# An attention and expert layer on one core: fewer counts for SP, and POOL's and VectorE's work around the last tiles laid out anew

## The chip, the core and the metric

One core of one Trainium2 chip runs the program. The metric is the device time of one execution in microseconds (us). The number to predict is the median for the changed kernel; for the kernel before it is 307.4 us.

## What is computed

x holds 2 x 1024 tokens of 256 numbers, the context 2 x 64 rows of 256, all in float32. The reference, cut to what matters:

```python
def attention(q_in, kv_in):            # 16 heads of 64; scores / sqrt(64), softmax over 64 keys
    q, k, v = q_in @ Wq + bq, kv_in @ Wk + bk, kv_in @ Wv + bv
    return softmax(q @ k.T / 8) @ v @ Wo + bo

def ffn(x):                            # 2048 tokens, 8 experts, 2 chosen for each token
    scores = sigmoid(x @ W_router)
    _, sel = top_k(scores + expert_bias, 2)
    w = scores[sel] / sum(scores[sel])
    shared = silu(x @ Wg_s) * (x @ Wu_s) @ Wd_s
    routed = [silu(x @ Wg[e]) * (x @ Wu[e]) @ Wd[e] for e in sel]
    return shared + sum(w * routed)

x = x + tanh(g_xattn) * attention(layernorm(x), ctx)
x = x + tanh(g_ffn) * ffn(layernorm(x))
```

The expert biases spread widely, so most tokens go to the same two experts.

## The kernel before

The tokens are 16 tiles of 128 rows. Each engine runs its own program; semaphores tie them. VectorE is `dve` (DVE), ScalarE `act`, TensorE `pe`, GpSimd `pool` (POOL), and SP issues most of the DMAs. An order of work is written out by hand on every engine.

**Start.** Wq and K are folded into matrices A and V and Wo into matrices B, one pair of heads after the other (`fold_v` on TensorE, L1392). V lies first in two PSUM banks, one for each half of the head pairs. `finish_v` adds the bias and copies it into `vT`: the first half on VectorE in two instructions (L988), the second on ScalarE in eight (L764), signalled by `v_done`. Each pair's B goes to SBUF as a high part (ScalarE, L736) and a low part (VectorE, L998). VectorE also makes the statistics of the first layer norm, in batches (`norm_stats`, L966 and L969).

**Token loop.** In step t the engines work on several tiles: scores of tile t + 2; row maximum and subtraction on VectorE (L1150, L1156), the exponential on ScalarE (L771), row sum and reciprocal of tile t + 1 on VectorE (L1140, L1144), multiplication with the reciprocal on POOL (L648), transposition and the attention product of tile t on TensorE, the second norm, and the shared expert of tile t - 2. Of the latter, `hidden(v)` gates the rows: for the tiles of `BY_POOL` (3 to 11) POOL does it from copies that ScalarE makes (L600, L602; the copies are L791 and L794), for the others VectorE from PSUM (L1095, L1098). In the step T - 3 = 13, VectorE's `choose(3)` picks the experts of tiles 9 to 11 after `hidden`; L1030 and L1031 are the smaller and the larger of two expert numbers.

POOL also scatters the normalized rows of each tile into the experts' areas in DRAM, twice per tile (`put_tile`, L612), from step 6 on; in step 13 it scatters tile 7, multiplies, gates tile 11 and scatters tile 8.

**Before the experts.** TensorE does the shared expert's down product of twelve tiles (`late_transpose`, `late_down`), among them `rank(6)`, a product for the totals and `count`. VectorE waits for these (L1051), fills `tables()` (which expert each of the 39 tiles of 128 slots belongs to, and what SP is to gather), gates tile 15 and makes the low parts of half of Wd (L1239); POOL had made the other half in the loop (L667).

**Experts.** Each engine runs 39 tiles, eight tiles unrolled in a hardware loop and the first and last steps written out. SP gathers the rows of tile j + 4 in step j (L504), after VectorE has written the scatter index of tile j (L1312); POOL scatters each tile's result to `routed_dram` (L691). When all tiles that hold rows of a part of the tokens are scattered, their results can be loaded. Four parts of four token tiles are loaded twice: plane 0 holds each token's result of the lower-numbered expert, plane 1 that of the higher (`load_plane`, L408, 512 KB each). How far the scatters must be for each of the eight loads is computed by VectorE in steps 1 and 2 (`last_turns`, `count_turns`), and SP reads it into registers, four for each load:

```python
for k, first in enumerate((4, 32)):
    if isinstance(j, int) and first <= j < first + T // PLANE:
        sp.wait_ge(chunk_turns_done, 1)
        turns.append(turn_values(chunk_turns[0:1, k, j - first, :]))
```

So steps 4 to 7 read the four rows of plane 0 and steps 32 to 35 the four of plane 1. At the end VectorE adds plane 0 (L1283, `add_low`) and plane 1 (L1331) for tiles 0 to 11, TensorE and ScalarE do tiles 12 to 15, and SP and ScalarE store (L402).

## Time and profile before

| | |
|---|---|
| median of 3 runs | 307.4 us (306.29 to 309.32) |
| the profiled execution, its own time | 309.48 us |
| its span in the profile | 307.7 us |
| mean granted clock of TensorE, share of full speed | 0.989 |
| TensorE matmul busy | 278.0 us (90%) |
| VectorE busy | 241.7 us (79%) |
| POOL busy | 170.0 us (55%) |
| ScalarE busy | 163.9 us (53%) |

The busy times say how much each engine has to do, not what sets the end. The chain of waits is followed back from the last instruction, at each step to what released it. A row in a timeline gives the start in us, how long it took (a merged row spans several instructions, their number behind the x), the engine, the line, what is written and read, and in brackets how long the engine was idle before and who ended that.

### The profile page before, as it was taken

Reading aid. Unit: us, or ns where it says so; the run is one execution under the profiler, and the core shown is the slowest. Engines: PE = TensorE matmul, PEld = TensorE weight load, DVE = VectorE, ACT = ScalarE, POOL = GpSimd, SP = SyncE. Lnnn points to the kernel's source line nnn. Section 1 sums busy time; section 2 is a strip of 40 time slices with the busy share of each in tenths; the row PEclk is TensorE's granted clock in tenths of the full one; section 3 lists DMA queues with packets and bytes.
Section 4 is the critical chain, followed back from the end, with each engine's and each line's share of the span. In section 5 each row is a group of like instructions: output and inputs, shape, how many; then the busy total and the mean of one; then the engine's idle time right before and its main releaser. Section 6 shows DMA issues by size and latency. Waiting matters only on the chain.

```text
span 307.7 us, 6608 instructions
## 1 busy us (share of the span) xinstructions
PE 278.0 (90%) x1746; PEld 248.8 (81%) x1747; DVE 241.7 (79%) x687; ACT 163.9 (53%) x426; POOL 170.0 (55%) x236
## 2 busy tenths in 40 slices
PE   2999979999999899999986969987799999999992
PEld 1788757898897798999876948876799899999881
DVE  0489869999999699989999575778877777777755
ACT  1462785666756566673653434744355565657611
POOL 8012216787757876897886775409553444444520
PEclk9999999999999999999998897999999999999999
DMA  6999994133379999713031122313244434343697
GB/s 186 367 295 318 269 293 119 47 90 94 102 207 292 306 315 325 223 36 105 35 104 37 53 87 88 90 53 105 69 123 126 118 92 121 113 129 105 223 344 264
DMA packets 45006, 49.74 MB, mean 162 GB/s; under 512 B 3928, under 2 KB 41650, under 8 KB 44978
## 3 DMA queue, kind: packets, MB, share of 16 engines
q1 hardware_dynamic: 39938, 39.37, 44.4%
q0 software_dynamic: 3408, 8.46, 8.1%
q10 hardware_dynamic: 1632, 1.57, 1.5%
q8 instruction: 13, 0.21, 0.3%
q14 instruction: 15, 0.12, 0.1%
HBM read 21.67 MB, written 28.64 MB: 163 GB/s over the span
## 4 chain that ended last, share of the span: by engine, by line
PE 47%; DVE 26%; issue 9%; DMA 6%; ACT 6%; POOL 3%; SPq 1%; DVEq 0%; ACTq 0%; POOLq 0%
PE bank L1404 5%; PE bank L1406 4%; PE bank L1405 4%; PE scores_ps L1404 4%; DVE probs L1156 4%; PE scores_ps L1406 3%; DVE pT_lo L1133 3%; DVE row_sum L1140 3%; PE scores_ps L1405 3%; PE bank L1350 3%; DMA Wk_sb<-in_L_xattn_Wk_dram 3%; DMA AB_free<-routed_dram 2%; DVE row_max L1150 2%; PE bank L1601 2%; PE scores_ps L1441 2%
## 5 line engine op out<-in xcount | busy, mean ns | idle before, releaser
L691 POOL DMA_INDIRECT routed_dram<-probs,sct_idx x39 | 38.0, 975 | 57.1 <-ACT probs L915 55.6
L648 POOL TENSOR_TENSOR probs<-probs,row_inv 128x1024 f32<-128x1024 f32 x16 | 30.5, 1908 | 25.2 <-DVE row_inv L1144 24.9
L612 POOL DMA_INDIRECT rows_dram<-xn,slot_i x32 | 32.0, 1001 | 14.6 <-issue 11.2
L1404 PE MATMUL bank<-AB_hi,pT_hi 128*128 128x256 f32 x128 | 37.7, 294 | 2.2 <-DVE pT_lo L1133 2.2
L1406 PE MATMUL bank<-AB_hi,pT_lo 128*128 128x256 f32 x128 | 36.5, 285 | 0.0
L1405 PE MATMUL bank<-AB_lo,pT_hi 128*128 128x256 f32 x128 | 36.4, 285 | 0.0
L771 ACT ACTIVATE probs<-probs 128x1024 f32<-128x1024 f32 x16 | 16.9, 1058 | 29.6 <-DVE probs L1156 29.6
L1404 PE MATMUL scores_ps<-AB_hi,xnT_hi 128*128 128x512 f32 x64 | 26.4, 413 | 1.8 <-DVE xnT_lo L1126 1.7
L1404 PEld LDWEIGHTS bank<-AB_hi,pT_hi 128*128 128x128 f32 x128 | 24.9, 194 | 2.7 <-issue 2.5
L1406 PE MATMUL scores_ps<-AB_hi,xnT_lo 128*128 128x512 f32 x64 | 25.3, 396 | 0.0
L1405 PE MATMUL scores_ps<-AB_lo,xnT_hi 128*128 128x512 f32 x64 | 25.3, 395 | 0.0
L1405 PEld LDWEIGHTS bank<-AB_lo,pT_hi 128*128 128x128 f32 x128 | 24.9, 194 | 0.0
L1406 PEld LDWEIGHTS bank<-AB_hi,pT_lo 128*128 128x128 f32 x128 | 24.8, 193 | 0.0
L1133 DVE TENSOR_TENSOR pT_lo<-bank,pT_hi 128x512 fp32r<-128x512 f32 x32 | 20.5, 682 | 1.8 <-ACT pT_hi L779 1.4
L1150 DVE TENSOR_REDUCE row_max<-scores_ps 128x16 f32<-128x1024 f32 x16 | 19.1, 1196 | 1.7 <-PE scores_ps L1406 1.6
L1302 DVE TENSOR_TENSOR xnT_lo<-bank,xnT_hi 128x256 fp32r<-128x256 f32 x39 | 16.6, 425 | 3.9 <-ACT xnT_hi L892 2.9
L1156 DVE TENSOR_TENSOR probs<-scores_ps,row_max 128x1024 f32<-128x1024 f32 x16 | 19.4, 1216 | 0.1
L1140 DVE TENSOR_REDUCE row_sum<-probs 128x16 f32<-128x1024 f32 x16 | 19.4, 1210 | 0.1
L830 ACT ACTIVATE xn2T_hi<-bank 128x256 fp32r<-128x256 f32 x16 | 6.2, 385 | 22.6 <-PE bank L1474 20.0
L1503 PE MATMUL bank<-ident,probs 128*128 128x128 f32 x128 | 16.9, 275 | 1.1 <-POOL probs L648 1.0
L779 ACT ACTIVATE pT_hi<-bank 128x512 fp32r<-128x512 f32 x32 | 17.2, 594 | 1.0 <-PE bank L1503 0.9
L1404 PE MATMUL bank<-W_hi,xnT_hi 128*128 x40 | 15.5, 387 | 2.0 <-DVE xnT_lo L1302 2.0
(249 smaller groups left out, 886.4 us busy)
## 6 DMA issues: line engine op xcount, KB each, us to landing
rows_dram<-pad_rows SPq DMA_DIRECT2D x10, 1040.0 KB, 15.8
rows_dram<-pad_rows SPq DMA_DIRECT2D x8, 780.0 KB, 12.5
AB_free<-routed_dram SPq DMA_DIRECT2D x8, 512.0 KB, 7.9
probs<-rows_dram SPq DMA_DIRECT2D x30, 130.0 KB
raw_buf<-in_L_ffn_Wg_dram SPq DMA_DIRECT2D x8, 192.0 KB, 2.5
raw_buf<-in_L_ffn_Wu_dram SPq DMA_DIRECT2D x8, 192.0 KB, 2.9
out_dram<-x_sb ACTq DMA_DIRECT2D x6, 256.0 KB, 2.7
pT_hi<-rows_dram SPq DMA_DIRECT2D x9, 130.0 KB
```

The costliest lines, as they stand in the source:

```text
L612: nc.gpsimd.indirect_dma_start(rows_dram[:, :], bass.IndirectOffsetOnAxis(ap=slot_i[:, t, k:k + 1], axis=0), xn2[:, t % KEEP, :], None).th ...
L648: nc.gpsimd.tensor_tensor(pr, pr, row_inv[:, :].unsqueeze(2).to_broadcast([P, H, KV]), ALU.mult).then_inc(norm_done, 1)
L691: nc.gpsimd.indirect_dma_start(routed_dram[:, :], bass.IndirectOffsetOnAxis(ap=sct_idx[(k - 2) % (2 * RING)][:, 0:1], axis=0), y_sb[ks][:, ...
L771: nc.scalar.activation(prob[m % 2][:, :], prob[m % 2][:, :], ACT.Exp).then_inc(exp_done, 1)
L779: nc.scalar.activation(pT_hi[:, 4 * h:4 * h + 4, :], pT_ps[h][:, :].rearrange("p (c s) -> p c s", c=4), ACT.Copy).then_inc(pT_hi_done, 1)
L1133: nc.vector.tensor_tensor(pT_lo[:, 4 * h:4 * h + 4, :], pT_ps[h][:, :].rearrange("p (c s) -> p c s", c=4), pT_hi[:, 4 * h:4 * h + 4, :].bi ...
L1140: nc.vector.tensor_reduce(row_sum[:, :], prob[m % 2][:, :].rearrange("p (h k) -> p h k", k=KV), AX_X, ALU.add).then_inc(sum_done, 1)
L1150: nc.vector.tensor_reduce(row_max[:, :], by_head, AX_X, ALU.max).then_inc(max_done, 1)
L1156: nc.vector.tensor_tensor(prob[u % 2][:, :].rearrange("p (h k) -> p h k", k=KV), by_head, row_max[:, :].unsqueeze(2).to_broadcast([P, H, KV]),
L1404: nc.tensor.matmul(out_ap, a_hi, b_hi, start=first, stop=False)
L1405: nc.tensor.matmul(out_ap, a_hi, b_lo, start=False, stop=False)
L1406: return nc.tensor.matmul(out_ap, a_lo, b_hi, start=False, stop=last)
```

## The change

Five edits:

1. SP keeps five rows of turns, not eight. The four of plane 0 are read in steps 4 to 7 as before. The readings of steps 32 to 35 are gone; the fifth row (the turn after which everything is scattered) is read after plane 0's third load and holds for all four loads of plane 1. `chunk_slots` and `chunk_turns` shrink to match.
2. VectorE computes these counts in steps 1, 2 and 3 of the experts and not in 1 and 2.
3. `BY_POOL` ends at tile 9: `hidden` of tiles 10 and 11 is VectorE's, from PSUM, and ScalarE's copies for them go. In step 13 `choose(3)` stands before `hidden`. POOL's scatters of tiles 7 to 9 move: in step 13 tile 7 and one half of tile 8 after the multiplication, then the other half in step 14 before it and tile 9 after it.
4. V's second half is VectorE's as well (`finish_v(1)`, two instructions), directly after the first; the third batch of statistics moves from there to a place after the row maximum of tile 1.
5. Before the experts: `rank(6)`, the totals and `count` stand ahead of `late_down(2)` on TensorE; `hidden(15)` stands ahead of the wait for the count on VectorE; the two late subtractions for Wd go from VectorE to POOL, after the tables.

```diff
-BY_POOL = range(3, 12)
+BY_POOL = range(3, 10)
...
-                for k, first in enumerate((4, 32)):
-                    if isinstance(j, int) and first <= j < first + T // PLANE:
-                        sp.wait_ge(chunk_turns_done, 1)
-                        turns.append(turn_values(chunk_turns[0:1, k, j - first, :]))
+                if isinstance(j, int) and 4 <= j < 4 + T // PLANE:
+                    sp.wait_ge(chunk_turns_done, 1)
+                    turns.append(turn_values(chunk_turns[0:1, j - 4, :]))
...
                     n = k * (T // PLANE) + c
+                    if n == T // PLANE - 1:
+                        turns.append(turn_values(chunk_turns[0:1, T // PLANE, :]))
                     for r in range(RING):
-                        sp.wait_ge(scattered[r], turns[n][r])
+                        sp.wait_ge(scattered[r], turns[min(n, T // PLANE)][r])
...
-                if 6 <= t < T - 2:
+                if 6 <= t < T - 3:
                     put_tile(t - 6)
                 if t == T - 2:
-                    put_tile(9, [0])
+                    put_tile(8, [1])
...
                 if t == T - 3:
-                    put_tile(8)
+                    put_tile(7)
+                    put_tile(8, [0])
                 if t == T - 2:
-                    put_tile(9, [1])
+                    put_tile(9)
...
+            pool.wait_ge(tile_row_done, 1)
+            for n in (2, 3):
+                part = slice(4 * n, 4 * n + 4)
+                pool.wait_ge(wd_hi_done, n + 1)
+                nc.gpsimd.tensor_tensor(Wd_lo[:, part, :], raw_d[n % 2][:, :, :, :].rearrange("p e k d -> p (e k) d"),
+                                        Wd_hi[:, part, :].bitcast(F32), ALU.subtract).then_inc(wd_lo_late, 1)
...
-            finish_v(1)
             high_x(2)
...
+                if t == T - 3:
+                    choose(3)
                 if inside(v) and v not in BY_POOL:
                     hidden(v)
-                if t == T - 3:
-                    choose(3)
...
             finish_v(0)
-            dve.wait_ge(ld_x[2], 16)
-            norm_stats(range(*NORMS[2]))
+            finish_v(1)
...
             max_rows(1)
+            dve.wait_ge(ld_x[2], 16)
+            norm_stats(range(*NORMS[2]))
             B_low([2])
...
             choose(6)
+            hidden(T - 1)
             dve.wait_ge(count_ps_done, 1)
             place(6, last=True)
             tables()
-            hidden(T - 1)
...
-                        pe.wait_ge(v_done, 2 * GC)
+                        pe.wait_ge(kv_done, 4 * NG)
...
-            late_down(2)
             rank(6)
             nc.tensor.matmul(last_ps, ones_r[:, :], mask[:, :, :].rearrange("p t e -> p (t e)"), start=True, stop=True)
             count(range(*BATCHES[6]), count_ps_done)
+            late_down(2)
```

The end of SP's program before, from the last row of turns on. `chunk_turns` are the counts, `AB_free` the planes; L487 is a reading of one value.

```order
L487 TENSOR_LOAD chunk_turns [waits chunk_turns_done]
L487 ISA x2
L487 TENSOR_LOAD chunk_turns
L487 ISA x2
L487 TENSOR_LOAD chunk_turns
L487 ISA x2
L487 TENSOR_LOAD chunk_turns
L487 ISA x2
L408 DMA AB_free<-routed_dram 128x4x256 [waits scattered2,scattered3,scattered1,scattered0] x4
L408 DMA AB_free<-routed_dram 128x4x256 [waits scattered3,scattered2,late_added,scattered1,scattered0] x4
L402 DMA out_dram<-x_sb 128x2x256 [waits plane1_added] x2
```

Now, from the last gather on (the numbers of the lines are almost the same there).

```order
L504 DMA probs<-rows_dram 128x260
L408 DMA AB_free<-routed_dram 128x4x256 [waits scattered2,scattered3,scattered1,scattered0] x3
L487 TENSOR_LOAD chunk_turns
L487 ISA x2
L487 TENSOR_LOAD chunk_turns
L487 ISA x2
L487 TENSOR_LOAD chunk_turns
L487 ISA x2
L487 TENSOR_LOAD chunk_turns
L487 ISA x2
L408 DMA AB_free<-routed_dram 128x4x256 [waits scattered2,scattered3,scattered1,scattered0]
L408 DMA AB_free<-routed_dram 128x4x256 [waits scattered3,scattered2,late_added,scattered1,scattered0] x4
```

The readings no longer stand between the last gather and the loads; four remain, behind the third load.

POOL from the multiplication of step 12 to that of step 13, before.

```order
L648 TENSOR_TENSOR probs<-probs,row_inv 128x1024 [waits inv_done]
L600 TENSOR_TENSOR gate_act<-tanh_g,late_hid 128x192 [waits plus_one_done,h_read,hid_done]
L602 TENSOR_TENSOR late_hid<-gate_act,late_hid 128x192 [waits gact_done]
L667 TENSOR_TENSOR AB_lo<-raw_buf,AB_hi 128x512 [waits wd_hi_done]
L626 TENSOR_TENSOR ve<-mv,eps_col 128x1 [waits xn2_done,mv2_done]
L627 TENSOR_TENSOR neg_mean<-mv,minus_one 128x1
L629 TENSOR_TENSOR rstd<-ve,minus_half 128x1 [waits ln2_step]
L631 TENSOR_TENSOR shift<-neg_mean,rstd 128x1 [waits ln2_step]
L612 DMA rows_dram<-xn,slot_i 16512x260 [waits filled2,xn2_done,payload_done,slot_done]
L612 DMA rows_dram<-xn,slot_i 16512x260 [waits xn2_done]
L648 TENSOR_TENSOR probs<-probs,row_inv 128x1024 [waits inv_done]
L600 TENSOR_TENSOR gate_act<-tanh_g,late_hid 128x192 [waits plus_one_done,h_read,hid_done]
```

The same stretch now (L649 is the multiplication, L613 the scatter).

```order
L649 TENSOR_TENSOR probs<-probs,row_inv 128x1024 [waits inv_done]
L668 TENSOR_TENSOR AB_lo<-raw_buf,AB_hi 128x512 [waits wd_hi_done]
L627 TENSOR_TENSOR ve<-mv,eps_col 128x1 [waits xn2_done,mv2_done]
L628 TENSOR_TENSOR neg_mean<-mv,minus_one 128x1
L630 TENSOR_TENSOR rstd<-ve,minus_half 128x1 [waits ln2_step]
L632 TENSOR_TENSOR shift<-neg_mean,rstd 128x1 [waits ln2_step]
L649 TENSOR_TENSOR probs<-probs,row_inv 128x1024 [waits inv_done]
L613 DMA rows_dram<-xn,slot_i 16512x260 [waits filled2,xn2_done,payload_done,slot_done]
L613 DMA rows_dram<-xn,slot_i 16512x260 [waits xn2_done]
L613 DMA rows_dram<-xn,slot_i 16512x260 [waits filled3,xn2_done,payload_done,slot_done]
L627 TENSOR_TENSOR ve<-mv,eps_col 128x1 [waits xn2_done,mv2_done]
```

The gating (L600, L602) is gone, and the two scatters stand behind the second multiplication.

VectorE at the start, around the row maximum of tile 1, before.

```order
L998 SCALAR_TENSOR_TENSOR AB_lo<-bank,tgate,AB_hi 128x2x256 [waits B_hi_done,gates_done]
L1150 TENSOR_REDUCE row_max<-scores_ps 128x16 [waits sub_done,scores_done]
L998 SCALAR_TENSOR_TENSOR AB_lo<-bank,tgate,AB_hi 128x2x256 [waits B_hi_done,gates_done]
L1156 TENSOR_TENSOR probs<-scores_ps,row_max 128x1024 [waits max_done]
L998 SCALAR_TENSOR_TENSOR AB_lo<-bank,tgate,AB_hi 128x2x256 [waits B_hi_done,gates_done]
L998 SCALAR_TENSOR_TENSOR AB_lo<-bank,tgate,AB_hi 128x2x256 [waits B_hi_done]
```

And now (L994 is the low part of B, L1146 the maximum, L962 and L965 the statistics).

```order
L994 SCALAR_TENSOR_TENSOR AB_lo<-bank,tgate,AB_hi 128x2x256 [waits B_hi_done,gates_done]
L1146 TENSOR_REDUCE row_max<-scores_ps 128x16 [waits sub_done,scores_done]
L962 BN_STATS stats<-x_sb 128x6 [waits ld_x2]
L962 BN_STATS stats<-x_sb 128x6 x2
L965 BN_AGGR mv<-stats 128x2 [waits stats1_done] x3
L994 SCALAR_TENSOR_TENSOR AB_lo<-bank,tgate,AB_hi 128x2x256 [waits B_hi_done,gates_done]
L1152 TENSOR_TENSOR probs<-scores_ps,row_max 128x1024 [waits max_done]
L994 SCALAR_TENSOR_TENSOR AB_lo<-bank,tgate,AB_hi 128x2x256 [waits B_hi_done,gates_done]
```

The three statistics stand between the maximum and the low part of pair 2.

## Rows read from the trace of the kernel before

**Rows 1.** The page, part 4: the chain, share of the span by engine.

```profile
PE 47%; DVE 26%; issue 9%; DMA 6%; ACT 6%; POOL 3%; SPq 1%; DVEq 0%; ACTq 0%; POOLq 0%
```

**Rows 2.** The chain in order of time, 28 to 50 us: start, us, what.

```profile
35.77 0.24 ACT vT L764
```

**Rows 3.** Timeline, 28 to 41 us: start, us, engine, line, op, [idle before].

```profile
27.98 1.37 DVE L988 TENSOR_TENSOR vT<-bank,bias_cols 64x512 f32<-64x512 f32 x2
...
29.38 1.08 DVE L966 BATCH_NORM_STATS2 stats<-x_sb 128x6 f32<-128x256 f32 x3
...
30.38 0.30 DVE L969 BATCH_NORM_AGGREGATE mv<-stats 128x2 f32<-128x6 f32 x3
...
35.67 3.07 ACT L764 ACTIVATE vT<-bank,bias_cols 64x128 f32<-64x128 f32 x8
...
36.75 1.21 DVE L1150 TENSOR_REDUCE row_max<-scores_ps 128x16 f32<-128x1024 f32 x1
...
39.96 0.75 DVE L998 SCALAR_TENSOR_TENSOR AB_lo<-bank,tgate,AB_hi 128x512 fp32r<-128x512 f32 x1 [1.99 <-ACT AB_hi L736]
```

**Rows 4.** Timeline of POOL, then DVE, 156 to 170 us; last, line L1030 alone.

```profile
159.21 1.92 POOL L648 TENSOR_TENSOR probs<-probs,row_inv 128x1024 f32<-128x1024 f32 x1
...
156.88 0.25 DVE L1144 RECIPROCAL row_inv<-row_sum 128x16 f32<-128x16 f32 x1
...
158.71 2.46 DVE L1030 TENSOR_TENSOR bank<-top_e 128x3 f32<-128x3 uint32 x1
...
161.71 1.21 DVE L1150 TENSOR_REDUCE row_max<-scores_ps 128x16 f32<-128x1024 f32 x1
...
168.66 0.29 DVE L1095 SCALAR_TENSOR_TENSOR gate_act<-tanh_g,bank 128x192 f32<-128x192 f32 x1
168.99 0.35 DVE L1098 TENSOR_TENSOR late_hid<-gate_act,bank 128x192 f32<-128x192 f32 x1
...
L1030 DVE TENSOR_TENSOR bank<-top_e x7: 168/172/2459, 87.4 to 187.6; 128x3 f32<-128x3 uint32 x4, 128x1 f32<-128x1 uint32 x2, 128x2 f32<-128x2 uint32 x1
```

**Rows 5.** Timeline, 186 to 203 us; ahead of it line L667 alone.

```profile
L667 POOL TENSOR_TENSOR AB_lo<-raw_buf,AB_hi x4: 1286/1288/1298, 128.1 to 153.9; 128x512 fp32r<-128x512 f32 x4
...
189.82 0.17 DVE L1051 TENSOR_TENSOR hot_val<-hot,bank 128x16 f32<-128x16 f32 x1 [1.51 <-PE bank L1453]
...
196.32 2.35 DVE L1239 TENSOR_TENSOR AB_lo<-raw_buf,AB_hi 128x1024 fp32r<-128x1024 f32 x2
...
201.80 0.38 PE L1601 MATMUL bank<-ident,probs 128*128 128x128 f32 x2
```

**Rows 6.** Timeline of SP, 274 to 294 us, and one row of DVE.

```profile
274.95 6.22 SPq L504 DMA_DIRECT2D probs<-rows_dram  x3
286.17 7.42 SPq L408 DMA_DIRECT2D AB_free<-routed_dram  x8
...
278.95 0.21 DVE L1312 SCALAR_TENSOR_TENSOR sct_idx<-probs,tile_e 128x1 int32<-128x1 f32 x1
```

**Rows 7.** The chain in order of time, 283 us to the end.

```profile
284.89 3.99 DMA routed_dram<-probs,sct_idx
...
288.97 7.35 DMA AB_free<-routed_dram
```

**Rows 8.** Timeline of DVE, 292 us to the end.

```profile
292.86 0.29 DVE L1103 TENSOR_TENSOR pT_lo<-bank,pT_lo 64x128 fp32r<-64x128 f32 x1
296.35 1.67 DVE L1331 SCALAR_TENSOR_TENSOR x_sb<-AB_free,weight,x_sb 128x256 f32<-128x256 f32 x4 [3.19 <-DMA AB_free<-routed_dram]
...
302.69 1.67 DVE L1331 SCALAR_TENSOR_TENSOR x_sb<-AB_free,weight,x_sb 128x256 f32<-128x256 f32 x4
```

**Rows 9.** Tile AB_free, landings; then the DMA view of 284 to 304 us.

```profile
DMA to landing us min/median/max: 5.2/7.9/9.2
...
GB/s 180 82 0 0 66 144 88 326 367 326 350 311 335 287 295 338 295 291 379 377 385 349 350 328 324 334 348 338 349 312 330 377 363 297 272 358 350 313 88 348
...
out_dram<-x_sb ACTq DMA_DIRECT2D x6, 256.0 KB, 2.7
```

43 lines of the change are left out of this document (16 added, 27 removed).

## The prediction, made before the changed kernel had run

> **What bounds the kernel now.** I read the chain by engine first: half of the span's chain is TensorE and a quarter VectorE [rows 1], so no engine alone sets the end and a saving counts only where its own piece of the chain is. The chain in order of time therefore decides. Four places of it touch the change.
>
> At 35.77 us the chain runs through ScalarE's V copies [rows 2]: eight of them hold ScalarE for 3.07 us, and VectorE idles 1.99 us in front of the low part at 39.96 us for a high part that ScalarE makes only after them [rows 3].
>
> In step 13 of the token loop VectorE is the chain. One 128x3 minimum of `choose(3)` (L1030) takes 2.46 us, from 158.71 to 161.17; POOL's multiplication of the probabilities (L648) runs from 159.21 to 161.13, and both end together [rows 4]. The row maximum behind it starts at 161.71.
>
> Between the token loop and the experts VectorE idles 1.51 us for the count of TensorE, then makes the tables, then two low parts of Wd in 2.35 us; the third tile's transposition starts at 201.80 [rows 5]. VectorE's late work there is behind the tables and TensorE is busy with the late products all the while, so it is not on the chain.
>
> The end: SP issues its last gathers from 274.95 to 281.17 us, and its first plane load only at 286.17 [rows 6]. What the first plane loads wait for was there long before. Counting the routing of the reference's own inputs, the experts get 1943, 28, 2048, 0, 0, 0, 0 and 77 rows, thus 16, 1, 16 and 1 tiles, 34 of the 39; plane 0's four loads need 21, 25, 29 and 33 tiles, and each of plane 1's four needs all 34. So only SP's reading of turns stands between the gathers and the loads: eight readings in 5.00 us, 0.62 us each. Plane 1's first load is issued at 288.97, when the scatter that was started at 284.89 has landed, and lands 7.35 us later [rows 7]. VectorE is ready for it at 293.15, waits 3.19 us, and then adds without a gap: 296.35 to 304.36 [rows 8]. In that time the DMA engines move some 335 GB/s almost from the first plane load on [rows 9]: plane 1 lands late because 2.1 MB of plane 0 are ahead of it.
>
> **The change part by part**, against the profiled execution (309.48 us, of which 307.7 are span; the median of the runs shown is 307.4, and I carry the sum over to it).
>
> SP's turns. All three steps of 32 to 35 lose their readings: sixteen of them go (10 us of SP's time), four come back as row 5, behind plane 0's third load. The last gather needs the index that VectorE writes at 278.95 + 0.21 = 279.16 [rows 6]; so the gathers end near 279.6 and the first three loads of plane 0 (each 0.52 MB, at 335 GB/s 1.57 us, together 4.7 us) go out about 6 us earlier and have landed by some 287. The four readings of row 5 (2.5 us, until 283.8) are covered, since plane 0's fourth load needs tile 33, whose scatter lands one tile before 288.9. Plane 1's first load cannot start before 288.97: both ways its count is 34. What is new is that the queue ahead of it holds at most the fourth load. A store of half the size takes 2.7 us from issue to landing [rows 9], of which 0.8 is the moving at 335 GB/s; so 0.52 MB alone take 1.9 + 1.57 = 3.5 us, and it lands at 292.5. VectorE is free at 293.15 only, so its adds start 296.35 - 293.2 = 3.15 us earlier. Bounds: nothing, if landing takes 7.35 us again; 2.15, if it takes the shortest of the eight (5.2 us, 294.2) [rows 9]; 3.2 at most, because then VectorE's own work ends it. I take **-3.1**, since the bytes ahead are what made it long. What follows is the same 20 adds and the same last stores, and those of TensorE's and ScalarE's tail move by as much.
>
> V on VectorE. Two instructions for the second half cost what the first two did, 1.37 us, and stand where three statistics stood (1.08 + 0.30 = 1.38) [rows 3]: nothing before the first row maximum moves. The statistics go behind the second maximum, which ends at 36.75 + 1.21 = 37.96; with 1.38 more VectorE reaches the low part at 39.3 instead of 39.96. ScalarE has lost 3.07 us, so its high part should be there. **-0.6**; bounds nothing (the high part still late) and -1.99 (all of the idle time).
>
> The gated rows of tiles 10 and 11. VectorE gets two instructions a tile, 0.29 + 0.35 and their gaps, 0.72 us [rows 4], once in step 12 and once in step 13; ScalarE loses two copies and POOL two products in each. Step 12 is a VectorE-bound round, so +0.7. In step 13 POOL now multiplies before it scatters: it can start once the reciprocal of 156.88 is there, later by the 0.7, so near 157.9, and ends near 159.8. `choose(3)` reaches L1030 at 158.71 + 0.7 = 159.4 and is held 0.4 us, not 2.3. Added: +0.7 + 0.7 - 2.0 = -0.6. POOL's scatters of tiles 7 to 9 then crowd toward step 15 by some tenths, and TensorE's idle time after rank(3) changes little. I take **-0.4**; bounds -2 (the gated rows fall into idle time) and +1.4 (the stall stays).
>
> Why the 128x3 minimum waits is a matter of a shared port. Both its inputs lie in SBUF. The Trainium skill (SBUF — State Buffer, "Who interferes with whom") says that such an instruction contends with a GpSimd instruction that reads SBUF, and that the one issued first keeps the port to its end. The trace agrees on the end (161.17 against 161.13) but not on the order: VectorE's began 0.5 us before POOL's. By the rule VectorE would have gone first and the stall would be chance; by the row it belongs to POOL's next instruction. With either the new order leaves 0.4.
>
> Before the experts. TensorE's rank and count go ahead of `late_down(2)`, so VectorE's idle 1.51 us takes in the gated rows of tile 15 and the tables end about 0.6 us sooner; TensorE's late products themselves stay, so this is worth nothing by itself. The Wd subtractions on POOL: its halves took 1.29 us for 512 columns [rows 5], so 1024 take at most 2 x 1.29 = 2.58, two 5.2. They wait for the tables, which end before VectorE's gated rows (0.7) and its own subtractions of 196.32, and now 0.6 sooner: from about 195.0 to 200.2. TensorE asks for them ahead of the transposition of 201.80: 1.6 us in hand, cost nothing, or up to 1 us if the port slows POOL. Behind them in POOL's queue are only the late adds, and nobody waits for those before the planes.
>
> Counts over three steps: nine instructions in steps 1 and 2 become nine in 1, 2 and 3. SP wants them at step 4. Half of what leaves steps 1 and 2 comes back in step 3, where VectorE waits for ScalarE anyway: **-0.1**, between -0.5 and +0.3.
>
> Sum: -3.1 - 0.6 - 0.4 - 0.1 = -4.2. That is 305.3 for an execution like the profiled one, and for the median 307.4 - 4.2 = **303.2 us**.
>
> **The rivals.**
> 1. The tail gives less: plane 1's four loads share the engines and the first lands as late as before. For it: they are issued close together, and 7.35 us is the only value seen for this load. Against it: then four loads were ahead. With 7.35 the tail gives nothing, 307.4 - 1.1 = 306.3; with 5.2 it would be 304.2.
> 2. The stall in step 13 stays, because POOL's other work (three scatters behind the multiplication) holds the port as well. Then the loop costs +1.4 and not -0.4: 303.2 + 1.8 = 305.0. Against it: of seven such minima only this one took over 0.2 us or so (the median is 0.172) [rows 4].
> 3. Slower: the early loads of plane 0 hold up the last tiles' scatters. The scatter of tile 34 took 3.99 us; if the 4.7 us of plane 0's bytes were ahead of it, it would land at 293.6, plane 1's first load would land at 293.6 + 7.35 = 301.0 in place of 296.3, and the end would be 4.7 - 1.1 = 3.6 us later: 311.0. It decides when more than about a third of these bytes still lie ahead at 284.89. Against it: they were issued from 279.7 and should be nearly through, and in the trace of before three loads were issued 1.3 us after that scatter without spoiling it.
> 4. The change does not do what it says: SP's readings stay between gathers and loads. The order excludes it.
>
> **How the numbers follow.** Forecast 0.68, rival 1 0.17, rival 2 0.10, rival 3 0.05. The range: below, the sum with V at -1.0, the loop at -1.4 and the tail at -3.2, 301.2; above, it reaches to rival 1, which with its noise I cut at 306.2. One per cent of 307.4 is 3.1 us, about what a measurement of this kernel can tell from no change: faster by more needs under 304.3. The forecast lies 1.1 below that, and the runs shown scatter by 3 us, so nine tenths of its chance count as faster, and a part of rival 1; rival 2 is no change. Faster 0.69, same 0.27, slower 0.04.
>
> **What would show it.** SP's first plane load near 279.7, a gap of 0.6 us from the last gather; VectorE's wait at L1331's new line near nothing, at about 292; L1030's successor at 0.5 us or less; no idle time over 1.5 us before the low part near 39; TensorE without a wait for POOL at 200. If the sum of the tail is under 1.5 us, or the step from 152 to 172 us is longer than before, the forecast is wrong.

## The result and the profile after

Twenty executions of each kernel: before 308.44 us median (306.29 to 309.47), changed 305.95 us (304.95 to 309.23). The ratio of the two is 0.9929, 95% interval 0.991 to 0.9948, so 2.2 us faster (1.6 to 2.8), where 4.2 were forecast. The time lies inside the range of 301.2 to 306.2, by a quarter of a microsecond, but 2.75 us above the forecast of 303.2. One of these comes from the start: the median of three runs (307.4) was a microsecond under the one of twenty. The forecast gave 0.69 to a gain of over one per cent (under 304.3) and 0.27 to no such change; the second came. Half of the expected gain was eaten, and this part is about by what.

VectorE's rows at the start, after the change:

```profile
36.63 0.67 DVE L994 SCALAR_TENSOR_TENSOR AB_lo<-bank,tgate,AB_hi 128x512 fp32r<-128x512 f32 x1
37.25 1.23 DVE L1146 TENSOR_REDUCE row_max<-scores_ps 128x16 f32<-128x1024 f32 x1
38.39 1.07 DVE L962 BATCH_NORM_STATS2 stats<-x_sb 128x6 f32<-128x256 f32 x3
39.37 0.30 DVE L965 BATCH_NORM_AGGREGATE mv<-stats 128x2 f32<-128x6 f32 x3
39.59 0.73 DVE L994 SCALAR_TENSOR_TENSOR AB_lo<-bank,tgate,AB_hi 128x512 fp32r<-128x512 f32 x1
```

The idle 1.99 us of [rows 3] is gone; the statistics fill 1.2 of it. The first row maximum came at 31.28 and not 30.71, but it varies by more than that without the V part too (below). In step 13 (VectorE, then POOL):

```profile
150.10 1.22 DVE L1146 TENSOR_REDUCE row_max<-scores_ps 128x16 f32<-128x1024 f32 x1
...
158.94 0.45 DVE L1026 TENSOR_TENSOR bank<-top_e 128x3 f32<-128x3 uint32 x1
```

```profile
157.45 1.91 POOL L649 TENSOR_TENSOR probs<-probs,row_inv 128x1024 f32<-128x1024 f32 x1 [2.46 <-DVE row_inv L1140]
```

The minimum takes 0.45 us where [rows 4] had 2.46. The end, SP, then VectorE, then TensorE's last products before and after:

```profile
278.42 11.60 SPq L408 DMA_DIRECT2D AB_free<-routed_dram  x8
299.26 1.17 SPq L402 DMA_DIRECT2D out_dram<-x_sb  x2
```

```profile
292.02 1.67 DVE L1328 SCALAR_TENSOR_TENSOR x_sb<-AB_free,weight,x_sb 128x256 f32<-128x256 f32 x4 [0.38 <-DMA AB_free<-routed_dram]
...
298.36 1.66 DVE L1328 SCALAR_TENSOR_TENSOR x_sb<-AB_free,weight,x_sb 128x256 f32<-128x256 f32 x4
```

```profile
300.91 0.70 PE L1445 MATMUL bank<-AB_free,late_hid 128*128 128x256 f32 x2 [1.18 <-DMA AB_free<-routed_dram]
...
302.31 0.59 PE L1445 MATMUL bank<-AB_free,late_hid 128*128 128x256 f32 x2
```

```profile
297.67 1.03 PE L1442 MATMUL bank<-AB_free,late_hid 128*128 128x256 f32 x4
...
299.40 0.59 PE L1442 MATMUL bank<-AB_free,late_hid 128*128 128x256 f32 x2
```

The first plane load is issued at 278.42 (286.17 in [rows 6]) and the adds start at 292.02 (296.35 in [rows 8]). Counted from the last scatter index (287.51 before, 285.99 now), VectorE's last add ends 14.03 us later where it was 16.84, but TensorE's last product 14.0 us later where it was 15.4: before, VectorE ended last by 1.5 us; now both end level. So each place that the forecast named did what it said, and the time still went elsewhere. Two views show where to look. TensorE's rows in front of the last rank (line 1459 is `rank(6)`'s first product, 1438 `late_down`):

```profile
185.59 0.38 PE L1431 MATMUL bank<-ident,late_hid 128*96 128x128 f32 x2
186.88 0.27 PE L1459 MATMUL bank<-mask,upper 128*128 128x8 f32 x1 [0.91 <-DVE mask L1038]
```

And the windows of 160 to 190 us, before and then after (columns: length, busy PE, PEld, DVE, ACT, POOL, granted clock of TensorE, DMA share, GB/s):

```profile
160.00:175.00 15.00, 11.27 (x73) 10.39 (x72) 11.71 (x28) 5.12 (x14) 10.82 (x17) 0.89 0.11 40
175.00:190.00 15.00, 11.99 (x68) 10.22 (x67) 9.26 (x54) 5.71 (x17) 10.25 (x14) 0.89 0.26 90
```

```profile
160.00:175.00 15.00, 12.62 (x75) 11.83 (x74) 10.94 (x27) 5.38 (x15) 10.35 (x16) 0.77 0.15 55
175.00:190.00 15.00, 11.67 (x72) 9.87 (x72) 11.29 (x65) 5.96 (x20) 11.23 (x16) 1.00 0.26 90
```

A mean of 0.89 over 15 us is 3.4 us at the lower of TensorE's two levels (1.2 GHz); 0.77 is 6.9 us. Such stretches are 3.4 us long here, or twice that, and how many fall, and where, differs between executions of one kernel, so a pair of traces must first be compared on them. The table does that for the profiled executions of all kernels with a whole tail. Its times are differences of starts in VectorE's timeline: the first to the third row maximum, the 14th to the 15th, the 15th to the 16th, the 14th to the first scatter index; then from the last scatter index to the end of the span. "Low" counts the 3.4 us stretches between 155 and 200 us; where there is one, it begins at 164.6 to 166.3, where there are two, the second begins at 181 to 185, or one of double length stands for both (changed, from 165.1; order only, from 180.4).

| kernel | 1st to 3rd | 14th to 15th | 15th to 16th | 14th to index | low | tail |
|---|---|---|---|---|---|---|
| before | 18.35 | 7.74 | 11.78 | 58.22 | 2 | 20.19 |
| changed | 17.40 | 8.33 | 10.48 | 57.37 | 2 | 18.21 |
| changed, again | 17.41 | 8.34 | 10.47 | 56.89 | 1 | 18.75 |
| turns only | 18.33 | 7.73 | 11.79 | 55.43 | 0 | 18.51 |
| old turns | 17.40 | 8.33 | 10.47 | 56.89 | 1 | 20.71 |
| V only | 17.40 | 7.74 | 11.78 | 56.26 | 1 | 20.29 |
| rows only | 18.36 | 8.33 | 10.47 | 57.16 | 2 | 20.89 |
| order only | 18.36 | 7.74 | 9.74 | 57.20 | 2 | 22.28 |
| late moves only | 18.39 | 7.74 | 11.76 | 56.32 | 0 | 21.57 |
| late product back | 17.40 | 8.34 | 10.46 | 55.97 | 1 | 18.66 |
| POOL's order | 17.40 | 8.34 | 10.47 | 56.90 | 2 | 18.54 |
| one row back | 17.40 | 7.74 | 10.40 | 54.92 | 1 | 17.94 |

The first row maximum itself stands anywhere from 29.06 to 31.64 us in these, with and without the V part; the loads of the first 30 us are the likely cause, which no run singles out. The place of a stretch counts as well: in three runs of the tail below, whose token loop is the changed kernel's, the way from the 14th row maximum to the first index is 57.9 us with one stretch from 180 to 182 us on, against 56.89 with one at 165, and 57.87 with both. So two rows of the table compare well only where number and place are alike. For the pair of the first two rows the pieces add up: +0.57 at the start, -0.95, -0.04 (third to 14th), -0.85, -0.25 (between the first and the last index), -1.98, together the 3.5 us between the spans 307.7 and 304.2. The profiled execution of before was the slowest of its twenty, which is most of why the pair says 3.5 and the ratio 2.2.

### The profile page after: what moved, and what is told of

Same layout as the page of the kernel before. It is cut to its first block, busy times and chain, and to the rows that moved or that the text cites. A ratio compares the mean times of both kernels' runs of the same rounds, so it can differ in the third digit from the quotient of the medians.

```text
span 304.2 us, 6562 instructions
## 1 busy us (share of the span) xinstructions
PE 277.8 (91%) x1746; PEld 249.2 (82%) x1747; DVE 239.6 (79%) x691; ACT 159.8 (53%) x414; POOL 172.9 (57%) x234
## 4 chain that ended last, share of the span: by engine, by line
PE 54%; DVE 26%; issue 7%; ACT 5%; POOL 3%; DMA 3%; SPq 1%; DVEq 0%; ACTq 0%; POOLq 0%
PE bank L1401 6%; PE bank L1403 5%; PE bank L1402 5%; PE scores_ps L1401 4%; PE scores_ps L1403 4%; PE scores_ps L1402 4%; DVE pT_lo L1129 4%; DVE probs L1152 4%; DVE row_sum L1136 3%; PE bank L1347 3%; DVE row_max L1146 3%; DMA Wk_sb<-in_L_xattn_Wk_dram 3%; PE bank L1598 2%; PE scores_ps L1438 2%; PE bank L1438 2%
## 5 line engine op out<-in xcount | busy, mean ns | idle before, releaser
L649 POOL TENSOR_TENSOR probs<-probs,row_inv 128x1024 f32<-128x1024 f32 x16 | 30.5, 1909 | 25.8 <-DVE row_inv L1140 25.6
L613 POOL DMA_INDIRECT rows_dram<-xn,slot_i x32 | 32.0, 1001 | 12.5 <-issue 10.5
L1299 DVE TENSOR_TENSOR xnT_lo<-bank,xnT_hi 128x256 fp32r<-128x256 f32 x39 | 16.5, 424 | 8.1 <-ACT xnT_hi L888 7.1
L1146 DVE TENSOR_REDUCE row_max<-scores_ps 128x16 f32<-128x1024 f32 x16 | 19.2, 1200 | 1.6 <-PE scores_ps L1403 1.6
L1401 PEld LDWEIGHTS scores_ps<-AB_hi,xnT_hi 128*128 128x128 f32 x64 | 12.0, 188 | 6.8 <-DVE xnT_lo L1122 4.7
```

Source lines behind the costliest of these rows:

```text
L613: nc.gpsimd.indirect_dma_start(rows_dram[:, :], bass.IndirectOffsetOnAxis(ap=slot_i[:, t, k:k + 1], axis=0), xn2[:, t % KEEP, :], None).th ...
L649: nc.gpsimd.tensor_tensor(pr, pr, row_inv[:, :].unsqueeze(2).to_broadcast([P, H, KV]), ALU.mult).then_inc(norm_done, 1)
L1146: nc.vector.tensor_reduce(row_max[:, :], by_head, AX_X, ALU.max).then_inc(max_done, 1)
L1401: nc.tensor.matmul(out_ap, a_hi, b_hi, start=first, stop=False)
```

## The experiments

Every ratio is to the kernel before on the same chip. The expectations argue by theories. 1: the pieces of the profiled pair, with TensorE's tail as the new bound of the end. 2: the late product that was moved had covered a wait. 3: POOL's queue takes back what VectorE wins. 4: TensorE and VectorE hold the end together. 5: one gated row is better left on POOL. 6: the DMA engines hold the end as well. They count tiles from 0, so their row maximum 15 is the 16th here.

**Turns alone.** The kernel before with the first part of the change (five rows, `turns[min(n, T // PLANE)]`, `tiles_up_to`, `last_turns`, `count_turns`):

```diff
-                        sp.wait_ge(scattered[r], turns[n][r])
+                        sp.wait_ge(scattered[r], turns[min(n, T // PLANE)][r])
```

> The kernel before with the five rows of turns and the counts over three steps, nothing else. Theory 1 (TensorE's tail is the new bound): the experts end when they did, VectorE's first add of plane 1 starts some 2.8 us earlier (near 293.5), but TensorE's four late products and twelve sums run without a wait from the end of the experts, lose only their own wait of 1.18 us for plane 1, and the span is 2.0 us shorter (305.7), ratio near 0.9935. Rival 1 (the prediction's step: TensorE's and ScalarE's tail move with VectorE's adds): 2.8 to 3.1 us shorter (304.7), ratio 0.990 to 0.991. Rival 2 (the medians, not the profiled pair, are right, and the early plane loads cost the scatters of the last tiles something in most executions): 1 us or less, ratio 0.997, with the last scatter landing 0.6 us later than 3.99 us after its issue.

Ratio 0.9937 (0.9903 to 0.9971), 305.32 against 307.28 us. This is theory 1's number, though the interval touches the prediction's (0.990 to 0.991); the trace decides. The tail is 18.5 us, and from the last scatter index VectorE's adds end at 14.3 us (16.8 before), TensorE's products at 14.1 (15.4 before). Over the six profiles of the table with the old turns the tail is 20.2 to 22.3 us, mean 21.0, over the six with the new ones 17.9 to 18.75, mean 18.4: 2.0 us in the profiled pair, 2.5 in the means.

**Old turns, the rest as changed.**

> The changed kernel with the old eight rows of turns and counts over two steps. Theory 1: only the lead of the experts is left, 1.5 us (third tile's gather, transpositions and the scatters 1.5 earlier), VectorE waits again about 3.2 us for plane 1's first load, and the span is 1.5 us shorter than before (306.2), ratio near 0.995. The ratios of this run and of the turns alone multiply to that of the whole change. Rival: the lead is lost in the tail, since SP's readings and the plane loads set the end and do not start earlier: ratio 0.998 or more.

A miss by theory 1: ratio 1.0061 (1.0031 to 1.009), 309.38 us. Taken without its largest part the change is slower than before. The profiled execution was the fastest of its eleven (306.34 us, 3 us under their median), so its trace can't show the whole loss. It has the expected tail (20.71) and shows two losses ahead of it. V alone and this run have one low stretch each near 165 us, and from the 14th row maximum to the first index the one takes 56.26, the other 56.89, though VectorE won 0.7 of that in steps 12 and 13. TensorE, V alone first, then this run:

```profile
184.32 1.03 PE L1429 MATMUL scores_ps<-Wds,lhT 96*128 96x256 f32 x4
185.40 0.27 PE L1450 MATMUL bank<-mask,upper 128*128 128x8 f32 x1
...
195.57 0.60 PE L1589 MATMUL bank<-ident,probs 128*128 128x128 f32 x4
```

```profile
183.21 0.38 PE L1424 MATMUL bank<-ident,late_hid 128*96 128x128 f32 x2
184.51 0.27 PE L1452 MATMUL bank<-mask,upper 128*128 128x8 f32 x1 [0.92 <-DVE mask L1036]
...
195.59 0.60 PE L1591 MATMUL bank<-ident,probs 128*128 128x128 f32 x4
```

In the first the third late product stands in the wait for the last choice and costs nothing. In the second it stands behind the count: TensorE idles 0.92 us, and from the last rank (line 1450, here 1452) to the experts' first transposition it takes 11.08 us and not 10.17. POOL, same order (line 625 is the norm's first instruction, 647 the multiplication, 611 the scatter):

```profile
167.36 1.91 POOL L647 TENSOR_TENSOR probs<-probs,row_inv 128x1024 f32<-128x1024 f32 x1
169.44 1.01 POOL L611 DMA_INDIRECT rows_dram<-xn,slot_i  x1 [0.17 <-issue]
170.95 0.18 POOL L625 TENSOR_TENSOR ve<-mv,eps_col 128x1 f32<-128x1 f32 x1 [0.51 <-DVE mv L1106]
```

```profile
166.04 1.91 POOL L647 TENSOR_TENSOR probs<-probs,row_inv 128x1024 f32<-128x1024 f32 x1
168.12 1.01 POOL L611 DMA_INDIRECT rows_dram<-xn,slot_i  x1 [0.17 <-issue]
169.43 0.96 POOL L611 DMA_INDIRECT rows_dram<-xn,slot_i  x1 [0.30 <-issue]
170.41 0.20 POOL L625 TENSOR_TENSOR ve<-mv,eps_col 128x1 f32<-128x1 f32 x1
```

POOL's multiplication is 1.32 us ahead, its norm of tile 14 only 0.54, because a second scatter now stands between them. These two readings became theories 2 and 3.

**V alone.**

```diff
-            finish_v(1)
```

(on ScalarE; on VectorE it goes behind `finish_v(0)`, and the statistics behind `max_rows(1)`.)

> The kernel before with V's second half on VectorE and the statistics behind the second row maximum, nothing else. Theory 1: the low part near 39.96 no longer waits for ScalarE, row maxima from the third tile on are 0.4 us earlier, the rest keeps it: 0.4 us, ratio 0.9987. Rival (the first row maximum comes 0.5 us later because of this edit, as the trace of the changed kernel has it, and half of the gain is lost there): the first maximum at 31.3 and not 30.7. If the 0.5 was chance of one execution, the first maximum stands at 30.7 and the gain is 0.9 us, ratio 0.997.

Ratio 0.9987 (0.9958 to 1.0016), 306.84 us. The interval tells nothing; the trace does. From the first to the third row maximum it takes 17.40 us and not 18.35, in every kernel that has this edit and in none that has it not: -0.95. The first row maximum was at 30.0, so the 0.57 us by which it came later in the changed kernel's first profile don't belong to this edit.

**Steps 12 and 13 alone.**

```diff
-BY_POOL = range(3, 12)
+BY_POOL = range(3, 10)
```

with `choose(3)` ahead of the gated rows and POOL's new `put_tile` order.

> The kernel before with the gated rows of tiles 10 and 11 on VectorE, POOL's new order of scatters and the choice ahead of the gated rows in step 13, nothing else. Theory 1: row maximum 14 is 0.6 us later, the 128x3 minimum takes 0.45 and not 2.46 us, row maximum 15 is 0.7 us earlier than before, and the experts keep that: ratio 0.9977. Rival: the stall comes back at another instruction of VectorE, since POOL's multiplication is as long as before: row maximum 15 at 162.3 or later, ratio 1.000 to 1.003.

Ratio 1.0012 (0.9985 to 1.0038), 307.36 us. Both row maxima stand where theory 1 had them (+0.6, then -1.3), and no stall comes back on VectorE. Yet the kernel is no faster: what follows gives it back (see the order alone, below).

**The late moves alone.** `rank(6)` and the count ahead of `late_down(2)`, `hidden(T - 1)` ahead of the tables, both Wd subtractions on POOL.

> The kernel before with the last part alone: the last rank and the last count ahead of the third late product, the gated rows of tile 15 ahead of the tables, the two Wd subtractions on POOL. Theory 2 (found in the profile of the run without the new turns): with that late product behind the count nothing of TensorE's covers its wait for the last choice; it idles 0.9 us in front of the last rank and the eleven late products start that much later, so the third tile's transposition and the experts are 0.9 us later and this part alone makes the kernel slower: ratio near 1.003. Rival (the prediction's step): worth nothing, 1.000, since the late products themselves stay. A third reading: the Wd subtractions on POOL are late and TensorE waits for them at the first down product, which would show as a wait of TensorE for POOL near 200 us.

Ratio 1.0026 (1.0001 to 1.0051), 309.01 against 308.2 us. The row in question:

```profile
187.21 0.27 PE L1463 MATMUL bank<-mask,upper 128*128 128x8 f32 x1 [0.92 <-DVE mask L1048]
```

No low stretch fell between 155 and 200 us, as in the run with the turns alone, and between those two the way from the 14th row maximum to the first index is 56.32 against 55.43: +0.89. TensorE never waited for POOL's Wd, so the third reading falls.

**The late product back**, on the changed kernel:

```diff
+            late_down(2)
             rank(6)
             nc.tensor.matmul(last_ps, ones_r[:, :], mask[:, :, :].rearrange("p t e -> p (t e)"), start=True, stop=True)
             count(range(*BATCHES[6]), count_ps_done)
-            late_down(2)
```

> The changed kernel with the third late product back ahead of the last rank; all else as changed. Theory 2: TensorE's idle time in front of the last rank falls from 0.9 us to 0.2 or less, the first scatter index comes 0.8 to 0.9 us earlier, and the time is 0.8 us under that of the changed kernel in the same call (ratio to before 0.003 lower). Rival (the tables on VectorE's side set the first gather and so the start of the experts): no difference from the changed kernel.

Ratio 0.9913 (0.9879 to 0.9947), 304.95 us, where the changed kernel beside it had 306.18. The wait is gone:

```profile
185.44 1.03 PE L1438 MATMUL scores_ps<-Wds,lhT 96*128 96x256 f32 x4
186.51 0.27 PE L1459 MATMUL bank<-mask,upper 128*128 128x8 f32 x1
```

and 55.97 stands against the 56.89 of the changed kernel, both with one low stretch at 165.4 us: -0.92. Undone in one kernel and made alone in another, the move is worth the same 0.9 us. That is shown in the traces; the ratios agree with it and are too wide to show it alone.

**POOL's order**, on top of it:

```diff
                 if t == T - 2:
-                    put_tile(8, [1])
+                    put_tile(9, [0])
...
                 if t == T - 3:
                     put_tile(7)
-                    put_tile(8, [0])
+                    put_tile(8)
                 if t == T - 2:
-                    put_tile(9)
+                    put_tile(9, [1])
```

> As the run with the late product back, and POOL's scatters of tiles 8 and 9 laid out once more: both of tile 8 in step 13 (where POOL idles 2.0 us), one of tile 9 ahead of the multiplication in step 14 and only one behind it. Theory 3 (POOL's queue took back what VectorE won in step 13): in the changed kernel the second scatter behind the multiplication delays the norm of tile 14 by 0.8 us and that of tile 15 with it; with it gone POOL's norms of tiles 14 and 15 and the rank behind them come 0.8 us earlier, and with theory 2's 0.8 the time is 1.6 us under that of the changed kernel (ratio near 0.987). Rival (VectorE or TensorE set that stretch, POOL's queue is cover): same time as the run with the late product back alone.

Ratio 0.988 (0.9837 to 0.9924), 303.92 us. POOL:

```profile
166.42 1.92 POOL L649 TENSOR_TENSOR probs<-probs,row_inv 128x1024 f32<-128x1024 f32 x1
168.50 1.01 POOL L613 DMA_INDIRECT rows_dram<-xn,slot_i  x1 [0.17 <-issue]
170.07 0.18 POOL L627 TENSOR_TENSOR ve<-mv,eps_col 128x1 f32<-128x1 f32 x1 [0.56 <-DVE mv L1115]
```

From the multiplication to the norm it takes 3.65 us, in the changed kernel beside it 4.37 (166.47 to 170.84), and now the norm waits for the statistics, where before the statistics had waited for POOL: 0.7 us. That the whole kernel keeps it isn't shown: the step over the run before (303.92 from 304.95) is inside the intervals. The trace keeps it up to VectorE's last choice, 44.19 us after the 14th row maximum against 44.85 in the run without TensorE's identity products (below), which has the changed kernel's token loop and its two low stretches at the same places. The first index, though, is only 0.98 us earlier than there (56.89 against 57.87) for this order and the late product together, and the late product alone had given 0.92.

**The changed kernel again.**

> The changed kernel once more, beside the others on the same chip: ratio 0.993, as measured. If the number of low-clock stretches of TensorE between 160 and 190 us varies from execution to execution, this profile may show another count than the first one's (6.7 us at the lower level), and the step from row maximum 13 to the first scatter index will be shorter or longer by 0.8 to 2.5 us per stretch; if the stretches belong to the order of the work, it shows the same again.

Ratio 0.9939 (0.9912 to 0.9966), 306.18 us. One low stretch where the first profile had two in one piece: their number belongs to the execution. Span 302.7 and not 304.2.

**The tail.** Three kernels made from the changed one. Without TensorE's identity products:

```diff
-            for z in range(NB, T):
-                tail_sum(z, ident[:, :], x_sb[:, z, :])
```

> The changed kernel; TensorE's four identity products, which add x to tiles 12 to 15, are left out, 1.72 us of TensorE's tail. Theory 4 (TensorE's tail and VectorE's adds now end within 1.5 us of each other, either one holds the end): TensorE ends 1.7 us earlier, VectorE's adds end where they did, and from the last scatter index to the end of the span it is 18.1 to 18.6 us, no more than 0.5 less than the 18.2 to 18.75 of the changed order. Theory 1 (TensorE alone): 1.7 us less, 16.7 to 17.0.

VectorE's adds of tiles 8 to 11 on 2 columns (`w = slice(0, D if t < 8 else 2)`):

> The changed kernel; VectorE's eight adds of tiles 8 to 11 are made on 2 of 256 columns, so 3 us and more of its tail goes. Theory 4: TensorE's work then holds the end; from the last scatter index to the end 18.0 to 18.6 us. Rival (VectorE's adds alone set the end, as the prediction had it, and TensorE's tail is cover): 15 to 16 us.

And both:

> Both at once: the identity products left out and the adds of tiles 8 to 11 on 2 columns. Theory 4: now the end moves, by TensorE's 1.7 us, to 16.4 to 17.0 us from the last scatter index. Rival (the loads of plane 1 or the stores hold the end, whatever the engines do): no shorter than 18 us.

From the last scatter index to the end: 18.2, 18.9 and 18.0 us, the changed kernel 18.2 and 18.75. Their ratios (0.993, 0.9916, 0.9925) don't differ from its own either. As the whole account of the end, theories 1 and 4 fall: with both engines' work cut nothing moved by more than the 0.5 us that these profiles differ by, and in the run with both TensorE waits in front of the sums of plane 1:

```profile
296.92 0.70 PE L1444 MATMUL bank<-AB_free,late_hid 128*128 128x256 f32 x2 [1.31 <-DMA AB_free<-routed_dram]
```

The windows of the same run (columns as above, the DMA share is the last but one):

```profile
292.00:294.00 2.00, 2.00 (x12) 1.76 (x11) 1.46 (x4) 0.63 (x2) 0.79 (x1) 1.00 1.00 338
294.00:296.00 2.00, 1.62 (x8) 1.08 (x6) 2.00 (x6) 0.00 (x0) 0.27 (x1) 1.00 1.10 362
```

Plane 1's fourth load, issued at 288.94, lands at 296.9 with the DMA engines full. So two more, with half of plane 1's bytes in the same four loads:

```diff
-                    load_plane(sp, k, c * PLANE, PLANE, (plane1_loaded if k else plane0_loaded)[c])
+                    load_plane(sp, k, c * PLANE, PLANE // 2 if k else PLANE, (plane1_loaded if k else plane0_loaded)[c])
```

> The changed kernel; of plane 1 only two of every four tiles are loaded (half the bytes in the same four loads), and each sum of plane 1 takes one of the loaded tiles; the count of sums and their sizes stay. Theory 6 (in the tail the DMA engines hold the end: plane 1's four loads move 2.1 MB at some 340 GB/s, so the last one lands as late as TensorE and VectorE would be done): VectorE's wait ahead of its first plane 1 add is nearly gone, but TensorE and VectorE are there right behind, so from the last scatter index to the end of the span only 0 to 1 us go: 17.3 to 18.5. Rival (only the latency of the loads counts, not their bytes): as before, 18.2 to 18.75, with the wait of 0.4 to 1.7 us still there.

> The half plane 1 together with both short tails (no identity products, adds of tiles 8 to 11 on 2 columns). Theory 6: TensorE no longer waits for plane 1's fourth load (1.31 us in the run with both short tails) and the end moves by 1 to 2 us more: 16.0 to 17.0 us from the last scatter index, where both short tails alone gave 18.0. Rival (the output stores hold the end): 17.7 or more.

18.35 us with half the bytes alone (no wait of TensorE, VectorE's 0.53), which both readings allowed, and 16.5 us (303.2 - 286.7) with half the bytes and both tails short. The last is one profile, but it lies 1.5 us under every other tail, and it excludes that the stores alone hold the end. Theory 6 holds: plane 1's bytes, TensorE's products and VectorE's adds end within a microsecond or so of each other, and of the cuts made only the one of all three moves the end (bytes with one engine alone weren't tried). Behind TensorE's last product come in every profile some 4 to 5 us of ScalarE and the last stores. In the last run the DMA engines have room from 292 to 298 us:

```profile
294.00:296.00 2.00, 2.00 (x11) 1.76 (x10) 2.00 (x6) 0.36 (x2) 1.05 (x1) 1.00 0.57 188
296.00:298.00 2.00, 2.00 (x11) 1.77 (x10) 2.00 (x10) 0.17 (x1) 0.24 (x1) 1.00 0.47 156
```

**One row back**, on top of POOL's order:

```diff
-BY_POOL = range(3, 10)
+BY_POOL = range(3, 11)
```

> As the run with POOL's new order, and the gated rows of tile 10 back on POOL in step 12 (those of tile 11 stay on VectorE). Theory 5: VectorE's 0.6 us in step 12 go (row maximum 14 to 7.7 us after row maximum 13, not 8.3), the stall of step 13 does not come back (0.5 us or less), POOL's norm of tile 12 comes 0.9 us later without delaying anything, and the time is 0.6 us under that run. Rival (POOL's queue takes it back again, by the later norm or by a stall in step 13): the same or slower.

Ratio 0.9863 (0.9821 to 0.9905), 303.5 us: the 0.6 us of step 12 are back (7.74), and the 15th to the 16th stays at 10.40. As a whole 0.4 us under the run with POOL's order, which alone isn't significant. The trace says more: the first index comes 54.92 us after the 14th row maximum, 55.97 in the run with the late product back, both with one low stretch at the same place. POOL's order and the row together are worth 1.05 us, 0.66 of them at the 16th row maximum. This kernel beats both, before by 1.4% and, by the ratios of the changed one (0.9929, 0.9939), the changed one by 0.7%.

**The order alone**, the gated rows staying on POOL:

> The kernel before with POOL's new order and the choice ahead of the gated rows in step 13, the gated rows of tiles 10 and 11 staying on POOL. Theory 3: VectorE wins 2 us in step 13 (row maximum 15 at 9.8 us after row maximum 14 and not at 11.8), and POOL, which now has gated rows, three scatters and a norm in a row, gives nearly all of it back: norm of tile 14 and the rank behind it where they were, ratio 0.998 to 1.002. On the clock: the kernels with this part and the gated rows on VectorE have run at a mean granted clock of 0.987 to 0.991, those without at 0.992 to 0.994; if the order alone does it, this one is near 0.989, if the gated rows do, near 0.993.

Ratio 1.0003 (0.9983 to 1.0022). The whole stall goes (9.74 us and not 11.78), and the time shows nothing of it. VectorE writes the statistics at 168.16 and POOL takes them up 2.4 us later, out of its queue:

```profile
168.16 0.18 DVE L1120 BATCH_NORM_AGGREGATE mv<-stats 128x2 f32<-128x6 f32 x1
```

```profile
168.41 1.01 POOL L612 DMA_INDIRECT rows_dram<-xn,slot_i  x1 [0.17 <-issue]
169.73 0.96 POOL L612 DMA_INDIRECT rows_dram<-xn,slot_i  x1 [0.30 <-issue]
170.70 0.21 POOL L626 TENSOR_TENSOR ve<-mv,eps_col 128x1 f32<-128x1 f32 x1
```

Counted from the 14th row maximum, POOL's norm of tile 14 (the row at 170.70) starts after 29.20 us; with the turns alone it is 29.98, and no low stretch had come by then in either. So POOL's queue took 1.26 of VectorE's 2.04 us: theory 3 is right in kind and said too much with "nearly all". Where the other 0.8 us went isn't shown; this profile has 6.8 us at the lower clock from 180.43 on.

The same count shows what steps 12 and 13 do in the changed kernel. In the three profiles with its token loop and no low stretch by then (both tails short, and the two with half of plane 1) the norm of tile 14 stands at 30.53 to 30.55, and with the turns alone or the late moves alone at 29.98 and 29.97: 0.55 us later, though the 16th row maximum is 0.7 earlier. POOL, both tails short:

```profile
168.59 1.01 POOL L613 DMA_INDIRECT rows_dram<-xn,slot_i  x1 [0.17 <-issue]
169.91 0.96 POOL L613 DMA_INDIRECT rows_dram<-xn,slot_i  x1 [0.30 <-issue]
170.89 0.21 POOL L627 TENSOR_TENSOR ve<-mv,eps_col 128x1 f32<-128x1 f32 x1
```

With a low stretch near 165 the old order is as late (30.46 and 30.53; the new 30.52 to 30.54, 30.67 where the stretch is twice as long), so there the part costs POOL nothing.

On the clock, the mean granted clock of the order alone was 0.9918, nearer the kernels without this part, but its 12 executions alone don't settle that half.

## Why the prediction was right and wrong

The sum, step by step: forecast, then what the runs showed.

**The tail, -3.1; it is -2.0 to -2.5.** Right up to VectorE: first load 278.4 (forecast near 279.7), adds 2.8 us earlier against the experts, a wait of 0.4 us. (In the other five profiles of the table with the new turns the wait is 0.1 to 1.7 us, and the first load of plane 1 takes 4.3 to 5.8 us from its issue to the first add; the sum had 3.5.) The failing step is "What follows is the same 20 adds and the same last stores, and those of TensorE's and ScalarE's tail move by as much". They can't: TensorE's tail starts at the end of the experts, not at plane 1, and had only the wait of 1.18 us ahead of its last four products to lose (it ends 1.4 us earlier, VectorE 2.8); the later loads of plane 1 land at the rate of the DMA engines. The first load's landing was taken for that of all four.

**V, -0.6; it is -0.95.** Inside the bounds, and the mechanism as told. From the first row maximum to the low part it is 8.31 us and was 9.25: the statistics took 1.2 us at their new place and not 1.38.

**Gated rows and the stall, -0.4; it is -0.7 at the 16th row maximum and -0.3 at the experts.** The -0.3 is the step from V alone to the old turns (56.26 to 56.89) less the 0.9 of the next part, one low stretch each, at places 1.7 us apart. Without a low stretch near 165 POOL's norm is 0.55 us later than before, so there the part may well cost time. The cause was read rightly: +0.6 in step 12, -1.3 in step 13, minimum at 0.45 us for a forecast of 0.4. The sentence that "POOL's scatters of tiles 7 to 9 then crowd toward step 15 by some tenths" was there, and it got no price. It is the norm of tile 14 that stands behind them, and VectorE's last choice starts 13.3 to 13.7 us behind that norm in all profiles without a low stretch near 180.

**Before the experts, 0; it is +0.9.** An error as large as the tail's, and the one that experiments isolate. "TensorE's late products themselves stay, so this is worth nothing by itself" counts instructions and not where they stand: the third late product had been the cover of TensorE's wait for VectorE's last choice. By the prediction's own view, in which TensorE is busy with late products until the transposition of 201.80 [rows 5], a microsecond of idle time opened ahead of them is a microsecond on the path. The second half was right: POOL's Wd (4.7 us for a forecast of 5.2) was waited for by nobody.

**Counts, -0.1; it is -0.2** (first to last index 87.10 to 86.85; first to third 3.93 to 3.94 us in every profile with the old counts, 3.71 to 3.72 in every one with the new).

Together -2.3 (tail, between its two readings) - 0.95 - 0.3 + 0.9 - 0.2 = -2.85, where the measurement says -2.2 (1.6 to 2.8). Some tenths are left. Part may be the gated rows in executions without a low stretch near 165, as said. They agree with a lower clock too: over all timed executions the mean granted clock was 0.9884 and 0.9900 for the changed kernel, for seven other kernels with both gated rows on VectorE (all but the two with half of plane 1, of two executions each) 0.9870 to 0.9900 (0.9907 with one row back on POOL); for the four sets of before 0.9922 to 0.9943, and for the four kernels with both rows on POOL 0.9918 to 0.9942. Within the four sets of before an execution with 0.001 less is 0.04 to 0.16 us longer (within the others it varies more), so 0.004 would be worth 0.2 to 0.6 us, an estimate. What in those rows does it wasn't found. One run stays outside the sum: the old turns with the rest as changed should be 0.35 us faster than before and measured 1.9 slower (1.0 to 2.8); its clock, the lowest but one (0.9871), accounts for 0.2 to 0.8 of that, and over a microsecond is open. Its two executions at a mean clock of 0.994 took 306.3 and 306.6 us, under before's median, and the nine at 0.981 to 0.989 took 307.9 to 310.1; only one of the two was profiled.

The lower end of the range, 301.2, isn't quite its terms: V at -1.0, the loop at -1.4 and the tail at -3.2 give 5.6, with -0.1 for the counts 301.7, and only with their bound of -0.5 301.3.

**The rivals.** Rival 1 (the tail gives less) was right in kind and for the most part not in cause: the first load didn't take 7.35 us again. From issue to the first add it was 4.0 us in the changed kernel, and 5.8 in its second profile. Rival 2 fell, the stall went; but its idea that POOL's queue keeps what VectorE wins was right one step later. Rival 3: tile 34's scatter landed 4.6 us after its start in the changed kernel and 3.99 before (283.36 to the loads at 287.96, against [rows 7]), about a tenth of its price, and over all profiles plane 1's first load is issued no later behind the last index with the new turns (1.1 to 2.1 us) than with the old (1.4 to 2.4). Rival 4 fell.

## What to carry to other kernels

A piece of work that can be moved for nothing may be the one that fills another's wait; before moving it, look at what its engine waits for next, and at what stands at that place afterwards. When a stall goes, price the next engine's queue in the same breath: here POOL's queue took back 1.3 of VectorE's 2.0 us in one kernel and at least 0.4 of its 0.7 in the other. And when a transfer comes earlier, ask for each engine of the tail where its own start comes from; three ends level with one another have to be cut together.

## What the runs showed of the hardware

TensorE's granted clock falls to the 1.2 GHz level in stretches of 3.4 us (6.8 in two profiles), beginning between 164 and 168 us and between 180 and 185, in some executions none, in some two, and this is part of what one trace of a kernel says: without any, the way from the 14th row maximum to the first index takes 55.43 us, with one at 166 us 56.26, with two 58.22, for the same order of that part. For the changed kernel's order it is 56.89 with one at 165, and 57.9 with one at 181, whether or not there is one at 165 too: here the later one decides. Around the first fall TensorE waits 2.24 us for VectorE (before, until 166.88, the fall at 167.58); but it waited just as long in the executions without a fall (until 165.18 with the turns alone), so the wait doesn't tell them apart.

The minimum of two columns against POOL's multiplication: in all seventeen profiles the one in step 13 ends 0.03 to 0.04 us after POOL does, also where it had begun 0.5 us before it (157.01 and 157.51 in the run with V alone, ends 159.47 and 159.43). Beside a scatter of POOL the next minimum of the same line, 128x2, takes 0.17 us (order alone, 173.07 within 172.45 to 173.49), and so does one of 128x1 beside a short 128x1 instruction of POOL (half of plane 1, 179.56 to 179.73 within 179.18 to 179.76), so not every overlap holds it. By the rule of the Trainium skill (SBUF — State Buffer, "Who interferes with whom") the one issued first keeps the port; the ends agree with it. The starts agree in the thirteen profiles with POOL's new order, where POOL began 1.5 us first; in the four with the old one they don't, and no run here told why.
